# GpSimd's wait for TensorE's count of one-hot groups, in the two weighted gather stages of a four-layer graph network

## What is computed

```
h = relu(layernorm(x))
m = h[src] * edge_weight                     # one row of 64 floats for each edge
ft = segment_sum(m, dst, 12500)              # layer 1: the weighted sum
x = x + ft @ W0.T + b0
# layer 2: segment sum, maximum and mean of edge_attr by src; needs count[src]
# layer 3: relation layer on h[src], divided by count[dst]
# layer 4: attention on h[src]
```

## Time and profile before

| | |
|---|---|
| median of 3 runs | 20154.68 us (20152.43 to 20169.36) |
| span of the profiled execution | 20183.3 us |
| first weighted stage, GpSimd's gathers | 81.9 to 1694 us |
| second weighted stage, VectorE's chunks | 7075 to about 10050 us |
| GpSimd busy | 13618.7 us, 67% of the span |
| VectorE busy | 8578.8 us, 43% |
| TensorE busy (matmul) | 2490.0 us, 12% |
| granted TensorE clock, mean | 0.534 |

### The profile page before, as it was taken

The page is one execution under the profiler, slowest core; times in us unless marked ns, Lnnn a source line. Parts: engine busy times, 40 slices in busy tenths (PEclk is TensorE's granted clock), DMA queues, the critical chain, the costliest instruction groups (busy, mean ns, idle before and its releaser), DMA issues. The chain is left out here.

```text
span 20183.3 us, 69907 instructions
## 1 busy us (share of the span) xinstructions
PE 2490.0 (12%) x17889; PEld 2157.0 (11%) x17889; DVE 8578.8 (43%) x7106; ACT 2766.6 (14%) x1894; POOL 13618.7 (67%) x13469
## 2 busy tenths in 40 slices
PE   1212222222222211111150000000000000000000
PEld 0111222222222200000130000000000000000000
DVE  5666677677677566666621111111113222222223
ACT  0000101101000022222221111111110111111110
POOL 5665566666666666666537777777776777777775
PEclk7555555555555555555575555555555555555555
DMA  3111111111111133333321111111113222222221
GB/s 72 45 41 53 49 50 55 52 50 53 54 50 50 42 106 100 100 100 98 94 71 48 47 47 47 47 47 47 47 46 34 48 48 48 48 48 48 48 48 41
DMA packets 613752, 1142.94 MB, mean 57 GB/s; under 512 B 331103, under 2 KB 383040, under 8 KB 571200
## 3 DMA queue, kind: packets, MB, share of 16 engines
q0 software_dynamic: 430432, 388.76, 10.9%
q10 hardware_dynamic: 34560, 436.30, 5.3%
q1 hardware_dynamic: 148704, 317.25, 5.0%
HBM read 617.82 MB, written 523.59 MB: 57 GB/s over the span
## 5 line engine op out<-in xcount | busy, mean ns | idle before, releaser
L787 POOL DMA_INDIRECT by_src<-H,sort_place_i x3240 | 3146.9, 971 | 1992.3 <-DVE sort_place_i L857 1020.2
L403 POOL DMA_INDIRECT rel_G<-rel_table,rel_idx x3240 | 3475.6, 1073 | 1311.7 <-issue 1031.8
L403 POOL DMA_INDIRECT att_G<-att_table,att_idx x3240 | 3418.0, 1055 | 1095.0 <-issue 1095.0
L403 POOL DMA_INDIRECT lead_rows<-h_table,wsum_idx x3120 | 2956.9, 948 | 1604.2 <-issue 939.1
L562 DVE SCALAR_TENSOR_TENSOR rel_Gf<-rel_Sf,rel_keep_first,rel_Gf 128x64 f32<-128x64 f32 x54 | 18.1, 335 | 4000.4 <-ACT rel_Gf L659 2094.3
L538 DVE TENSOR_TENSOR_SCAN att_near<-att_near,er_in 128x60 f32<-128x60 f32 x54 | 19.1, 354 | 3471.6 <-DMA att_G<-att_table,att_idx 3471.6
L934 PE MATMUL pG<-sort_cnt,sort_lowT 128*128 128x98 f32 x6480 | 1300.8, 366 | 882.7 <-DVE sort_prod L843 500.4
L439 DVE TENSOR_TENSOR wsum_low<-iota_b,wsum_parts 128x3840 fp8e4<-128x3840 bf16 x216 | 896.4, 4150 | 1103.6 <-remote 934.0
L934 PEld LDWEIGHTS pG<-sort_cnt,sort_lowT 128*128 128x128 f32 x6480 | 1181.7, 272 | 891.6 <-DVE sort_prod L843 505.2
L706 PE MATMUL wsum_C<-wsum_high,wsum_low 128*128 128x98 fp8e4 x6480 | 714.4, 266 | 3985.3 <-issue 2780.0
L843 DVE TENSOR_TENSOR sort_prod<-pG,sort_high 128x392 f32<-128x392 f32 x810 | 453.5, 565 | 1529.1 <-remote 1169.9
(11 more groups left out here) (389 smaller groups left out, 7825.7 us busy)
## 6 DMA issues: line engine op xcount, KB each, us to landing
scan_att<-att_S ACTq DMA_DIRECT2D x54, 1980.0 KB
scan_wsum<-wsum_S ACTq DMA_DIRECT2D x54, 1920.0 KB
sort_keys<-key_rows SPq DMA_DIRECT2D x54, 1920.0 KB
scan_pool<-pool_S ACTq DMA_DIRECT2D x72, 1440.0 KB
scan_rel<-rel_S ACTq DMA_DIRECT2D x54, 1920.0 KB
pool_row<-by_src SPq DMA_DIRECT2D x36, 1485.0 KB
sort_lows<-low_rows SPq DMA_DIRECT2D x54, 960.0 KB
sort_feat<-in_attr SPq DMA_DIRECT2D x54, 960.0 KB
```

The source lines that it names most:

```text
L403: pool.indirect_dma_start(out=G[s][:, j, :], out_offset=None, in_=table, in_offset=bass.IndirectOffsetOnAxis(ap=idx[s][:, j:j + 1], axis=0 ...
L787: pool.indirect_dma_start(out=by_src, out_offset=bass.IndirectOffsetOnAxis(ap=place_i[s][:, j:j + 1], axis=0), in_=row[s][:, j, :], in_off ...
```

## The change

One wait of GpSimd's is taken out. It stood in every chunk of the two weighted stages (`counts` is set only there). Nothing else changes: the same instructions, buffers, order on each engine, and the same wait of VectorE at line 436.

```diff
@@ -396,8 +396,6 @@
                     def gather(i, s):
                         pool.wait_ge(index_ready, 2 * i + s + 1)
                         pool.wait_ge(turned, 2 * i + s + 1)
-                        if counts:
-                            pool.wait_ge(oh_used, 2 * HG * i + (s * HG + 1 - (HG if pooled else 0)))
                         pool.sem_inc(issuing, 1)
                         for j in range(L):
                             pool.indirect_dma_start(
```

## The result

The changed kernel takes 20960.92 us (median of four runs, 20916.72 to 20989.76) against 20162.02 for the kernel before in the same session (20152.43 to 20169.49): 1.039 times as long, 95% interval 1.0376 to 1.0403. The predicted time was 20960.

What follows compares the result with a forecast made beforehand. Running gathers slow TensorE, which recovers only after they pause; without the wait, pauses return later through VectorE's chain. First stage +258 and second +550 make +808 us on 20154.7: 20960 us, range 20400 to 21250.

Steps and rivals of the forecast that it cites:

- fast stretches only in the long pauses: Weighted stages: TensorE's products come fast only while GpSimd stands in its long pauses, about 64 us first stage, 80 second.
- The pair: First stage: two gathers run on, then GpSimd stands; 214.9 us for two chunks against 182.6, a loss of 32.3.
- the three groups left: First stage: three of a side's six groups still to be built by VectorE after recovery, 3 x 7.2 = 21.6 us.
- 16.7 + 7.6: First stage: VectorE's own work of the next chunk, 16.7 us, then ScalarE's copy, store and index copy, 7.6 us.
- The recovery after four: Start of first stage: TensorE recovers after four gathers in a row, estimated 36 us by 9 us for each gather.
- the chain behind: Start of first stage: blocked groups, VectorE's own work, ScalarE's copies and GpSimd's start after recovery, 47 us.
- Threes: Second stage: three gathers run on before GpSimd is stopped; 305.2 us per three chunks against 255, with recovery 27.
- 11 cycles by 50: Second stage: 34 chunks gathered make 11 cycles of three, each losing 50 us, +550 us; bounds +450 and +650.
- A: Weighted stages: gathers don't make TensorE's slow stretches, so the pauses go; faster, 19526 us at best; chance 0.15.
- B: Weighted stages: the pause comes back at its old length, periods stay 91 and 85 us, no change; chance 0.05.
- C: Weighted stages: same mechanism but VectorE let through earlier, slower but less, +330 us, 20490 us; chance 0.10.
- The rule of the Trainium skill: Weighted loops: a taken branch outside the fetched window waits for a DMA; TensorE's slowness would hang on its loop's end.

Runs made afterwards that it cites:

- the last two runs: On another chip (kernel before 17321.57 us): changed kernel with 128 x 384 memset before each gather issue, 18262.81 us; kernel before, first-stage wait a side looser, 17318.43 us.

## Why the prediction was right

**What bounds the kernel.** TensorE is slow while gathers are issued and recovers after they stop: the windows show it again around a pair and around three, and with the products taken out of the second stage the wait is worth nothing. VectorE's wait, through which GpSimd is now stopped, stands in line 435 (not 436) of the kernel before. One sign did not come as stated, that TensorE would show fast stretches only in the long pauses: in the first gather of a pair it still does 106 products in 75 us, where the second has 27.

```profile
673.00:748.00 75.00, 12.80 (x106) 9.22 (x107) 0.00 (x0) 0.50 0.25 73
```

**First stage.** The pair was 214.9 by the sum and is 214.8; its pause 65 us where 64 was said. The terms hold one by one: recovery 18; then `Gf` 22.5 us after the release (21.6 for the three groups left); the issue after that at 1317.55, 24.1 later (16.7 + 7.6). The choice of three groups is in the rows too: the third group waited till 1214.95, the fourth till the recovery at 1271.02. The fifth gather starts at 458.13, said was 465. The recovery after four was put at 36, by a rule of 9 us a gather that stops after three, and is 27 to VectorE's release at 411.57; the last of the four gathers ended at 384 (382 in the sum), and the chain behind is 46.6 (47). So the start costs 25 us where 32 was said, and the seven pairs the 226 of the sum. Stage: +248 for +258.

**Second stage.** Threes, as predicted: 304.7 for 305.2, recovery 26 for 27, pause 79 for 80. The product of the sum, 11 cycles by 50, is less well borne out than its total. From the first gather after the scatter to the last one it is 3248 us, against 2803: +445, what nine threes of 49.7 cost, and nine is the number of pauses near 79 us. The other 101 us come from the start of the last gather to the first of `rel_G` (770.3 against 669.0): VectorE is further behind when the gathers end, and 91 us of that show as GpSimd's wait for `scan_pool` (142.1; 51.4 before). The prediction had no tail; it counted two cycles more, and the two came to the same. That the stage's +546.5 lies so near its +550 is luck in this respect.

**The rivals.** A needed products at 0.1 us beside gathers; they come at 2.75. B and C needed shorter blocked chains; the pairs and threes have the full one. Against A the prediction also argued that runs without an effect of the profiler would be without the waits, and so far below the span. Each timed run comes with a span and a granted clock of its own, so something of it was recorded as well, and the argument is empty. The rule of the Trainium skill that was weighed there ("Runtime: NRT & Kernel Launch", section "Instruction fetch mechanics") stays without support: the same loop, with its same taken branch, has no slow stretch on the chip of the last two runs (147 products in 50 us).

**What is shown and what is not.** Shown: the loss is in the two stages, adds up from them, hangs on TensorE's products, and comes as fewer and longer pauses released by VectorE and ScalarE. Shown: the limit acts on single instructions, in steps of 0.70 us, on GpSimd as well as on TensorE, goes by neither rows nor bytes, and is missing in the traces of one chip. Not shown: what it is made of. An untested candidate is the recording of the runs, in which each instruction of each engine has its entry; no run was made without it, and if it takes part, the 799 us hold for recorded runs only. It would not be the cause by itself, for the traces of the last chip were recorded too and have no limit. And the changed kernel was not run on that chip; since the wait stopped nobody there, its removal should change nothing there, which is argued only.

## What to carry to other kernels

A wait of 629 us in all on the busiest engine was what kept a slower engine near; taken out, it came back as 1.3 ms of waits with a longer chain in each. Before such a wait is removed, look for a place in the trace where the waiting engine already runs on without it, read there at what rate the other engine works and how long it takes to recover, and build the new cycle from those rows. Then look whether the same program on another chip shows the wait at all.

## What the runs showed of the hardware

- On the chips with the limit, GpSimd's indirect DMAs of 128 rows go out every 1.25 us (0.95 + 0.30) for about three gathers of 60, then every 1.40 on average. With 64 rows it is 1.21 us at first and the same limit later.
- While that limit is being approached TensorE gets a product per 2.75 us, a weight load and a product each taking a turn of mostly 1.40 us, at either granted clock (0.50 and 1.00). It stays slow for 8, 18, 26 and 27 us after the last issue of one, two, three and four gathers.
- A memset of 128 x 16 (0.13 us) or two semaphore steps between issues fit into the gap (interval 1.25 to 1.26 us), but the hold-ups then begin in the first gather, and a semaphore step, at the median 17 ns, can last 0.70 us (1906 of 6240). A memset of 128 x 384 takes 0.43 us and lengthens the interval to 1.55.
- The same kernel took 17321.57 us on one chip and 20162 to 20300 on the others. In its traces there the limit is missing in all stages, the relation and scatter stages included.
